# The load of w1 issued without a wait for x, and the low parts of all FFN weights made on GpSimd

## The chip, the cores and the metric

The kernel runs on one core of a Trainium2 chip. The metric is the device time of one execution in microseconds (us). Its engines are TensorE (PE in the profile), VectorE (DVE), ScalarE (ACT), GpSimd (POOL) and SyncE (SP); each works through its own list of instructions in order and waits on semaphores that the others raise. SP and ACT also issue DMA transfers, in order, from queues of their own (SPq, ACTq).

## The reference, cut to what matters

64 sequences ("tiles" below) of 128 tokens with 256 features go through gated cross attention (16 heads of 16, causal) and a gated FFN with a hidden width of 1024, of whose 16 blocks a router keeps 4 per token.

```python
def ffn(x, w_router, b_router, w1, b1, w2, b2):
    prob = softmax(xf @ w_router + b_router)
    mask = top 4 of the 16 blocks
    h = relu(xf @ w1b + b1b)
    y = einsum(h, w2b, mask) + b2
...
x = x + tanh(g_xattn[0]) * attention(_layernorm(x), ctx, ctx)
x = x + tanh(g_ffn[0]) * ffn(_layernorm(x), w_router, b_router, w1, b1, w2, b2)
```

All inputs are float32.

## The kernel before, in words

One tile is one sequence of 128 tokens. The work is a software pipeline over `ITERATIONS`, a loop variable i from -5 to 71 that every engine runs through on its own; "step i" below is one pass. The order on each engine is written out by hand, and semaphores tie the engines together.

In step i, PE makes the plain scores of tile i+1 (`scores`, L314), DVE takes their row maxima with a minus sign (`row_maximum`, L674 and L676), and these ride in `q_pad` of tile i+3 through PE's transpose (`q_transposed`, L283) and ACT's copy (`q_evacuated`, L504). SP moves them with two small DMAs into row 16 of each head's qT (`max_row`, L970). Then PE makes the scores of tile i again with the maximum subtracted (`shifted_scores`, L344), ACT takes the exponentials in two halves (`exponentials`, L525) and POOL zeroes what is above the diagonal (`causal_weights`, L873). Scores and shifted scores use the same four PSUM banks, so the next `scores` waits for the exponentials. `attention_out` (L357) and `out_transposed` (L371) follow one step later; DVE divides and adds the residual (`attention_added`, L684 to L694) and takes the statistics of the second layer norm. POOL makes the reciprocal roots of the variances, of x of tile i+4 and of the attention result of tile i-2 together (`roots`, L829 and L831). DVE normalises (`normalised`, L664, and `normalised_again`, L701, which makes `xn`), PE transposes `xn` (`x_transposed`, L382), ACT copies it to `xT` and, rounded, to `xT_high`, and DVE makes `xT_low` (`x_parts`, L707). Each second step has the router (L393, L401) with DVE's `route` (L746 to L758), ACT's `choice` (L569, `used`) and SP's transposing DMA of `used` (L1010).

The FFN matmuls are made from a rounded part ("high", type fp32r) and the rest ("low") of each operand, with three products: high by high, low by high, high by low. FFN work begins at step 5 (`hidden`, L423 to L425, then `ffn_out`, L446 to L448, from step 7).

The weights are split on the chip. w1 arrives by one DMA of 1 MB that ACT issues (L589). w2 arrives by eight DMAs on SP's queue (L1051) in the buffer that is later `hid`. They are cut into eight pieces of 128 x 512 elements, 0 to 3 of w1 and 4 to 7 of w2. ACT makes the high part of a piece by a copy (`weights_high`, L576), and then DVE (`weights_low`, L723) or POOL (`weights_low`, L887) the low part by a subtraction, in the step that `pieces_of` gives:

```python
def pieces_of(i):
    return {0: (0, 1), 1: (2, 3), 2: (4, 5), 3: (6,), 4: (7,)}.get(i, ())

W_LOW_BY_POOL = (0, 2, 4)
```

In POOL's loop `weights_low` comes behind `causal_weights` and `hidden_low`, at the end of a step, with `roots` of the next step behind it. In DVE's loop it comes behind `normalised_again` (steps up to 8) and before `layernorm_stats` of a later x. The first `hidden` on PE waits for four low parts, the first masked hidden piece on DVE (L738) and the first `ffn_out` for all eight.

x and the context stream in by DMAs of two tiles; at the start SP issues x of tiles 0, 1, 2 and 3 (L994 to L996), some small loads, then x of tiles 4 to 7 (L963).

Of the kernel before, what the change touches and what calls it, by code (L numbers as in the profile page):

```python
# [7 lines left out]
ALU = mybir.AluOpType  # L8
ACT = mybir.ActivationFunctionType
F32 = mybir.dt.float32  # L10
# [28 lines left out]
def build(nc, A_x, A_ctx, A_g_xattn, A_g_ffn, A_w_router, A_b_router, A_w1T, A_b1, A_w2T, A_b2, out):  # L39
# [24 lines left out]
    with ctx:  # L64
# [3 lines left out]
        def sem(name):  # L68
            return ctx.enter_context(nc.semaphore(name))
# [80 lines left out]
        x_landed = [sem(f"x_landed{i}") for i in range(XS // PAIR)]  # L150
# [30 lines left out]
        top_found, clipped_made, clipped_found, marked_made = (sem(n) for n in (  # L181
            "top_found", "clipped_made", "clipped_found", "marked_made"))

        w_low_also_made = sem("w_low_also_made")
        gated_b2_made, adding_made = sem("gated_b2_made"), sem("adding_made")

        ident16_zeroed, ident16_made, ident_zeroed, ident_made = (sem(n) for n in (
# [69 lines left out]
        def w_piece(n):  # L257
            turn = n % 4
            if n < 4:
                k, e = turn // 2, slice(turn % 2 * BLOCKS // 2, (turn % 2 + 1) * BLOCKS // 2)  # L260
                high, low = (t[:, k].rearrange("p c (e r) -> p e c r", e=BLOCKS)[:, e] for t in (w1_high, w1_low))
                return 0, w1_stage[:, k, e], high, low
            c = slice(turn * 2, turn * 2 + 2)
            return 1, w2_stage[:, c], w2_high[:, c], w2_low[:, c]

        def pieces_of(i):
            return {0: (0, 1), 1: (2, 3), 2: (4, 5), 3: (6,), 4: (7,)}.get(i, ())


        W_LOW_BY_POOL = (0, 2, 4)  # L270

        block = ctx.enter_context(nc.Block())

# [1 line left out]
        def _(pe):  # L275
# [128 lines left out]
            def hidden(p, m):  # L404
                ps = p % 2
                if m == 0:
                    pe.wait_ge(xT_low_made, p * PAIR + PAIR)
                if m == 0 and p == 0:
                    pe.wait_ge(k_copied, FFN_LAG + 2)
                    pe.wait_ge(w_low_made, 2)  # L410
                    pe.wait_ge(w_low_also_made, 2)
                n = PIECES * p + m
                if n > TAIL_PIECE:
                    pe.wait_ge(exp_done, 2 * N)
                    pe.wait_ge(hid_made, PC * (n - 1))
                elif n > 0:
                    pe.wait_ge(hid_made, PC * n)
                for j in range(PC):
                    c = PC * m + j
                    bank = hid_bank(n)[:, j * TOKS:(j + 1) * TOKS]  # L420
                    for k in range(KC):
                        high, low = (t[:, ps, k].rearrange("p t s -> p (t s)") for t in (xT_high, xT_low))
                        pe.matmul(out=bank, lhsT=w1_high[:, k, c], rhs=high, start=k == 0, stop=False)  # L423
                        pe.matmul(out=bank, lhsT=w1_high[:, k, c], rhs=low, start=False, stop=False)  # L424
                        made = pe.matmul(out=bank, lhsT=w1_low[:, k, c], rhs=high, start=False, stop=k == KC - 1)  # L425
                made.then_inc(hidden_made, 1)

            def ffn_out(b, half):
                p, t = divmod(b, PAIR)
                bank = out_bank(b)  # L430
                toks = slice(t * S, (t + 1) * S)
                if half == 0 and b >= TAIL_TILE:
                    pe.wait_ge(exp_done, 2 * N)
                    pe.wait_ge(y_made, b - 1)
                elif half == 0 and b >= 1:
                    pe.wait_ge(y_made, b)
                if half == 0 and b == 0:
                    pe.wait_ge(q_copied, QUERIES_BY_PE)
                    pe.wait_ge(w_low_made, 3)
                    pe.wait_ge(w_low_also_made, 5)  # L440
                if t == 0:
                    pe.wait_ge(h_low_made, PIECES * p + 2 * half + 2)
                for c in range(half * HC // 2, (half + 1) * HC // 2):
                    a, z = c == 0, c == HC - 1
                    high, low = h_high[:, p % 2, c, toks], h_low[:, p % 2, c, toks]
                    pe.matmul(out=bank[:, 0:D], lhsT=high, rhs=w2_high[:, c, :], start=a, stop=False)  # L446
                    pe.matmul(out=bank[:, 0:D], lhsT=high, rhs=w2_low[:, c, :], start=False, stop=False)  # L447
                    made = pe.matmul(out=bank[:, 0:D], lhsT=low, rhs=w2_high[:, c, :], start=False, stop=z)  # L448
                if half == 1:
                    made.then_inc(ffn_made, 1)  # L450
# [50 lines left out]
        def _(act):  # L501
# [83 lines left out]
            for u in range(U):  # L585
                rows = slice(u * PAD, (u + 1) * PAD)
                act.copy(tri[rows], triangle[rows, rows].unsqueeze(1).to_broadcast([PAD, HB, PAD])).then_inc(tri_made, 1)
            act.wait_ge(x_landed[1], 16)
            act.dma_start(w1_stage[:].rearrange("p k e c r -> p k (e c r)"),  # L589
                          A_w1T.rearrange("(k p) n -> p k n", p=P)).then_inc(w_landed[0], 16)  # L590
            def rest(i):
# [46 lines left out]
        def _(dve):  # L638
# [77 lines left out]
                dve.scalar_tensor_tensor(y_out[:, pair % 2, b % PAIR, :], out_bank(b)[:, 0:D], tanh_g[:, 1:2],  # L716
                                         x2_b2[:, b % GS, :], ALU.mult, ALU.add).then_inc(y_made, 1)

            def weights_low(i):
                for n in (n for n in pieces_of(i) if n not in W_LOW_BY_POOL):  # L720
                    _w, stage, high, low = w_piece(n)
                    dve.wait_ge(w_high_made, n + 1)
                    dve.tensor_tensor(low, stage, high.bitcast(F32), ALU.subtract).then_inc(w_low_also_made, 1)  # L723

            def hidden_masked(p, m):
                n = PIECES * p + m
                dve.wait_ge(hidden_made, n + 1)
                if n == 0:
                    dve.wait_ge(b1_landed, 16 * HC)
                    dve.wait_ge(w_low_made, 3)  # L730
                    dve.wait_ge(w_low_also_made, 5)
                if m == 0:
                    dve.wait_ge(used_turned, 16 * (p + 1))
                if n >= 4:
                    dve.wait_ge(h_low_made, n - 3)
                for j in range(PC):
                    c = PC * m + j
                    dve.scalar_tensor_tensor(hid[:, n % 4, j], hid_bank(n)[:, j * TOKS:(j + 1) * TOKS],  # L738
                                             b1_cols[:, c:c + 1], used_all[:, p % 2], ALU.add, ALU.mult
                                             ).then_inc(hid_made, 1)  # L740
# [33 lines left out]
            for i in ITERATIONS:  # L774
                pr, pu = router_pair(i), used_pair(i)
                p, m = hidden_pair(i)
                if 0 <= i - OUT_LAG - 1 < N:
                    finished(i - OUT_LAG - 1)
                if 0 <= i - 2 < N:
                    attention_added(i - 2)  # L780
                if 0 <= i + 3 < N:
                    normalised(i + 3)
                if 0 <= i + 1 < N:
                    row_maximum(i + 1)

                early = q_early(i)
                if early and 0 <= i - 2 < N:
                    normalised_again(i - 2)
                if p is not None:
                    hidden_masked(p, m)  # L790
                weights_low(i)
                if not early and 0 <= i - 2 < N:
                    normalised_again(i - 2)
                if 0 <= i + 5 < N:
                    layernorm_stats(i + 5)
                if i == FIRST + 1:
                    dve.wait_ge(place_zeroed, 1)
                    dve.wait_ge(ident16_made, 1)
                    places(0)
                    places(1)  # L800
                if 0 <= i - 3 < N:
                    x_parts(i - 3)
                if pr is not None:
                    route(pr)
                if i == FIRST + 2:
                    places(2)
                    places(3)
                if p is not None:
                    hidden_masked(p, m + 1)
                if i == FIRST + 2:  # L810
                    dve.wait_ge(ident_made, 1)
                    halves = ident[:].rearrange("p (t c e) -> p t c e", c=KC, e=PAD)
                    dve.tensor_tensor(adding[:], halves[:, :, 0], halves[:, :, 1], ALU.add).then_inc(adding_made, 1)
                if i == 0:
                    dve.wait_ge(small_landed, 16 * (KC + 1))
                    dve.wait_ge(tanh_done, 1)
                    dve.tensor_scalar(gated_b2[:], b2_all[:], tanh_g[:, 1:2], None, ALU.mult).then_inc(gated_b2_made, 1)

        @block.gpsimd
        def _(pool):  # L820
# [60 lines left out]
                                   ALU.subtract).then_inc(h_low_made, 1)  # L881

            def weights_low(i):
                for n in (n for n in pieces_of(i) if n in W_LOW_BY_POOL):
                    _w, stage, high, low = w_piece(n)
                    pool.wait_ge(w_high_made, n + 1)
                    pool.tensor_tensor(low, stage, high.bitcast(F32), ALU.subtract).then_inc(w_low_made, 1)  # L887
# [195 lines left out]
```

## Time and profile before

| | us |
|---|---|
| median of 3 runs | 681.2 |
| lowest, highest | 681.01, 684.17 |
| the profiled execution, its own time | 680.97 |
| its span | 679.1 |
| PE busy, share of the span | 659.7, 97% |
| DVE busy | 527.8, 78% |
| ACT busy | 538.9, 79% |
| POOL busy | 556.0, 82% |

The span is what the profiler sees from the first to the last instruction; the execution's own time holds a further 1.9 us around it. Busy shares are averages over the whole span. A row of a timeline gives start, duration, engine and line, the operation with its output and input, and in brackets how long the engine had been idle and what ended the idle time; a row with x2 holds two instructions in one. DMA issues are on SPq and ACTq. Line numbers are those of the kernel before.

### The profile page before, as it was taken

The page shows a single profiled execution, that of the slowest core. Times are in us where ns is not written, and L with a number is a line of the kernel's source. Part 1 is how long each engine was busy: PE and PEld are TensorE (multiplying, and loading weights), DVE is VectorE, ACT ScalarE, POOL GpSimd, SP SyncE. Part 2 cuts the span into 40 slices and gives each one's busy share as a digit, 9 for nine tenths or more (in the row PEclk, how much of TensorE's full clock was granted, in tenths as well). Part 3 has the DMA queues.
Part 4 walks back from the last instruction along what each step waited for, and adds up shares of the span by engine and source line. Part 5 has one row for each costly group of instructions (what it writes and reads, how often), then busy time and mean ns, then how long its engine had stood idle before and what let it go on. Part 6 is the DMA issues. An engine that isn't in the chain of part 4 may idle for free.

```text
span 679.1 us, 30579 instructions
## 1 busy us (share of the span) xinstructions
PE 659.7 (97%) x12960; PEld 611.9 (90%) x12960; DVE 527.8 (78%) x1429; ACT 538.9 (79%) x785; POOL 556.0 (82%) x718
## 2 busy tenths in 40 slices
PE   6779999999999999999999999999999999999997
PEld 5668899999999999999999999989999999999997
DVE  6899887788777778788778878777878877877742
ACT  4668788888888888888888888888888888887732
POOL 6677888988988898888898898888888889887643
PEclk9899999999999999999999999999999999999999
DMA  5323355556545446645556654544554554553110
GB/s 197 96 55 86 88 109 99 116 109 115 120 114 116 99 110 116 111 112 113 100 117 107 116 111 122 103 107 114 113 113 112 116 100 96 98 86 64 28 40 32
DMA packets 192279, 69.24 MB, mean 102 GB/s; under 512 B 166160, under 2 KB 191888, under 8 KB 192144
## 3 DMA queue, kind: packets, MB, share of 16 engines
q1 hardware_dynamic: 191312, 65.72, 45.7%
q8 instruction: 102, 1.67, 1.1%
q10 hardware_dynamic: 832, 1.57, 0.6%
q14 instruction: 33, 0.27, 0.1%
HBM read 19.03 MB, written 8.39 MB: 40 GB/s over the span
## 4 chain that ended last, share of the span: by engine, by line
PE 86%; DVE 5%; DMA 3%; ACT 2%; issue 2%; POOL 1%; SPq 1%; POOLq 0%; DVEq 0%
PE bank L423 11%; PE score_banks L344 10%; PE bank L357 8%; PE score_banks L314 8%; PE bank L425 8%; PE bank L424 8%; PE bank L446 8%; PE bank L447 8%; PE bank L448 8%; PE bank L371 4%; PE bank L401 2%; PE score_banks L327 1%; DMA used_all<-used 1%; PE bank L393 1%; ACT weights L525 1%
## 5 line engine op out<-in xcount | busy, mean ns | idle before, releaser
L880 POOL TENSOR_TENSOR h_low<-hid,h_high 128x512 fp32r<-128x512 f32 x128 | 164.2, 1283 | 12.8 <-ACT hid L560 12.8
L738 DVE SCALAR_TENSOR_TENSOR hid<-bank,b_cols,used_all 128x256 f32<-128x256 f32 x248 | 108.1, 477 | 65.9 <-PE bank L425 58.2
L873 POOL TENSOR_SCALAR_AFFINE_SELECT weights<-weights 128x1024 f32<-128x1024 f32 x128 | 138.2, 1103 | 18.2 <-ACT weights L525 16.4
L423 PE MATMUL bank<-xT_high,w_high 128*128 128x256 f32 x496 | 151.5, 305 | 0.8 <-DVE hid L738 0.7
L525 ACT ACTIVATE weights<-score_banks 128x1024 f32<-128x1024 f32 x128 | 124.3, 1024 | 34.7 <-PE score_banks L344 34.6
L424 PE MATMUL bank<-xT_low,w_high 128*128 128x256 f32 x496 | 139.4, 281 | 0.0
L425 PE MATMUL bank<-xT_high,w_low 128*128 128x256 f32 x496 | 139.4, 281 | 0.0
L446 PE MATMUL bank<-w_high,h_high 128*128 128x256 f32 x488 | 137.3, 281 | 0.7 <-POOL h_low L880 0.7
L447 PE MATMUL bank<-w_low,h_high 128*128 128x256 f32 x488 | 137.7, 282 | 0.0
L448 PE MATMUL bank<-w_high,h_low 128*128 128x256 f32 x488 | 136.2, 279 | 0.0
L423 PEld LDWEIGHTS bank<-xT_high,w_high 128*128 128x128 f32 x496 | 93.3, 188 | 8.9 <-DVE hid L738 1.1
L424 PEld LDWEIGHTS bank<-xT_low,w_high 128*128 128x128 f32 x496 | 93.5, 189 | 0.0
L425 PEld LDWEIGHTS bank<-xT_high,w_low 128*128 128x128 f32 x496 | 93.3, 188 | 0.0
L446 PEld LDWEIGHTS bank<-w_high,h_high 128*128 128x128 f32 x488 | 91.8, 188 | 0.9 <-POOL h_low L880 0.9
L448 PEld LDWEIGHTS bank<-w_high,h_low 128*128 128x128 f32 x488 | 92.2, 189 | 0.0
L447 PEld LDWEIGHTS bank<-w_low,h_high 128*128 128x128 f32 x488 | 91.8, 188 | 0.0
L519 ACT COPY kT<-kT_parts 128x1024 uint16<-128x1024 uint16 x57 | 77.9, 1366 | 16.1 <-DMA kT_parts<-k_parts 15.8
L559 ACT ACTIVATE h_high<-hid 128x512 fp32r<-128x512 f32 x128 | 80.8, 631 | 9.9 <-DVE hid L738 9.9
L344 PE MATMUL score_banks<-qT,kT 32*128 32x128 f32 x2048 | 75.1, 283 | 6.6 <-DMA qT<-qT 3.6
L513 ACT COPY qT<-qT_parts 128x1024 uint16<-128x1024 uint16 x57 | 77.6, 1361 | 4.1 <-DMA qT_parts<-q_parts 3.7
L344 PEld LDWEIGHTS score_banks<-qT,kT 32*128 32x128 f32 x2048 | 63.0, 186 | 19.6 <-issue 12.7
L560 ACT ACTIVATE hid<-hid 128x512 f32<-128x512 f32 x128 | 80.3, 628 | 0.0
(105 smaller groups left out, 1411.1 us busy)
## 6 DMA issues: line engine op xcount, KB each, us to landing
x_in<-in_x SPq DMA_DIRECT2D x31, 256.0 KB, 3.1
out_y<-y_out SPq DMA_DIRECT2D x31, 256.0 KB, 2.2
c_in<-in_ctx SPq DMA_DIRECT2D x30, 256.0 KB, 2.8
qT<-qT SPq DMA_DIRECT2D x128, 4.0 KB
w_stage<-in_w1T ACTq DMA_DIRECT2D x1, 1024.0 KB, 9.2
hid<-in_w2T SPq DMA_DIRECT2D x8, 128.0 KB, 2.7
kT_parts<-k_parts SPq DMA_TRANSPOSE x57, 2.8
qT_parts<-q_parts SPq DMA_TRANSPOSE x57, 2.7
```

The source lines that it names most:

```text
L344: made = pe.matmul(out=score_banks[:, u, cols], lhsT=kT[rows, s, cols], rhs=qT[rows, s, cols], start=True, stop=True, tile_position=(u * P ...
L423: pe.matmul(out=bank, lhsT=w1_high[:, k, c], rhs=high, start=k == 0, stop=False)
L424: pe.matmul(out=bank, lhsT=w1_high[:, k, c], rhs=low, start=False, stop=False)
L425: made = pe.matmul(out=bank, lhsT=w1_low[:, k, c], rhs=high, start=False, stop=k == KC - 1)
L446: pe.matmul(out=bank[:, 0:D], lhsT=high, rhs=w2_high[:, c, :], start=a, stop=False)
L447: pe.matmul(out=bank[:, 0:D], lhsT=high, rhs=w2_low[:, c, :], start=False, stop=False)
L448: made = pe.matmul(out=bank[:, 0:D], lhsT=low, rhs=w2_high[:, c, :], start=False, stop=z)
L525: act.activation(weights[:, b % 2, half * 2 * HB:(half + 1) * 2 * HB, :].rearrange("p h q -> p (h q)"), score_banks[:, 2 * half:2 * half + ...
L559: act.activation(h_high[:, p % 2, chunks], hid[:, n % 4], ACT.Relu)
L738: dve.scalar_tensor_tensor(hid[:, n % 4, j], hid_bank(n)[:, j * TOKS:(j + 1) * TOKS], b1_cols[:, c:c + 1], used_all[:, p % 2], ALU.add, AL ...
L873: pool.affine_select(out=w, in_=w, compare_op=ALU.is_ge, fill=0.0, base=0, pattern=[[0, 2 * HB], [1, S]], channel_multiplier=-1).then_inc( ...
L880: pool.tensor_tensor(h_low[:, p % 2, chunks], hid[:, n % 4], h_high[:, p % 2, chunks].bitcast(F32), ALU.subtract).then_inc(h_low_made, 1)
```

## The change

ACT issues the DMA of w1 without waiting for x of tiles 2 and 3. POOL makes all eight low parts. The pieces come in the order 1, 2, 2, 2, 1 over steps 0 to 4, for ACT's high parts too. The semaphore of DVE's low parts goes, and the waits for both semaphores become waits for one.

```diff
@@ -264,10 +263,8 @@
         def pieces_of(i):
-            return {0: (0, 1), 1: (2, 3), 2: (4, 5), 3: (6,), 4: (7,)}.get(i, ())
-
-
-        W_LOW_BY_POOL = (0, 2, 4)
+            return {0: (0,), 1: (1, 2), 2: (3, 4), 3: (5, 6), 4: (7,)}.get(i, ())
@@ -407,8 +404,7 @@
                 if m == 0 and p == 0:
                     pe.wait_ge(k_copied, FFN_LAG + 2)
-                    pe.wait_ge(w_low_made, 2)
-                    pe.wait_ge(w_low_also_made, 2)
+                    pe.wait_ge(w_low_made, 4)
@@ -436,8 +432,7 @@
                     pe.wait_ge(q_copied, QUERIES_BY_PE)
-                    pe.wait_ge(w_low_made, 3)
-                    pe.wait_ge(w_low_also_made, 5)
+                    pe.wait_ge(w_low_made, 8)
@@ -585,7 +580,6 @@
-            act.wait_ge(x_landed[1], 16)
             act.dma_start(w1_stage[:].rearrange("p k e c r -> p k (e c r)"),
@@ -716,19 +710,12 @@
-            def weights_low(i):
-                for n in (n for n in pieces_of(i) if n not in W_LOW_BY_POOL):
-                    _w, stage, high, low = w_piece(n)
-                    dve.wait_ge(w_high_made, n + 1)
-                    dve.tensor_tensor(low, stage, high.bitcast(F32), ALU.subtract).then_inc(w_low_also_made, 1)
-
             def hidden_masked(p, m):
...
-                    dve.wait_ge(w_low_made, 3)
-                    dve.wait_ge(w_low_also_made, 5)
+                    dve.wait_ge(w_low_made, 8)
@@ -788,7 +775,6 @@
-                weights_low(i)
@@ -881,7 +867,7 @@
             def weights_low(i):
-                for n in (n for n in pieces_of(i) if n in W_LOW_BY_POOL):
+                for n in pieces_of(i):
```

POOL's order from the masks of step 2 to those of step 4, before (`weights` are the exponentials that are masked, `ve` and `rstd` are made by `roots`, `x_b` is x2_b2, the residual with the gated bias):

```order
L873 AFFINE_SELECT weights<-weights 128x1024 x2
L887 TENSOR_TENSOR w_low<-hid,w_high 128x512
L829 TENSOR_SCALAR ve<-mv 128x2
L831 TENSOR_TENSOR rstd<-ve,half_power 128x2
L919 TENSOR_TENSOR x_b<-x,gated_b 128x256
L839 COPY v_pad<-c_in 128x16x16
L873 AFFINE_SELECT weights<-weights 128x1024 x2
L829 TENSOR_SCALAR ve<-mv 128x2
L831 TENSOR_TENSOR rstd<-ve,half_power 128x2
```

and the same stretch of the change:

```order
L859 AFFINE_SELECT weights<-weights 128x1024 x2
L873 TENSOR_TENSOR w_low<-w_stage,w_high 128x8x8x8
L873 TENSOR_TENSOR w_low<-hid,w_high 128x512
L815 TENSOR_SCALAR ve<-mv 128x2
L817 TENSOR_TENSOR rstd<-ve,half_power 128x2
L905 TENSOR_TENSOR x_b<-x,gated_b 128x256
L825 COPY v_pad<-c_in 128x16x16
L859 AFFINE_SELECT weights<-weights 128x1024 x2
L873 TENSOR_TENSOR w_low<-hid,w_high 128x512 x2
L815 TENSOR_SCALAR ve<-mv 128x2
L817 TENSOR_TENSOR rstd<-ve,half_power 128x2
```

One low part more stands before `roots` of step 3, and two before `roots` of step 4, where there were none. Step 1 also has one more before `roots` of step 2, and step 4 one where there was none.

DVE's order from the maxima of step 3 to the router of step 4, before:

```order
L676 TENSOR_REDUCE q_pad<-score_banks 128x4x2
L701 TENSOR_SCALAR xn<-x,mv,rstd 128x256
L723 TENSOR_TENSOR w_low<-hid,w_high 128x512
L645 BN_STATS stats<-x_in 128x6
L647 BN_AGGR mv<-stats 128x2
L707 TENSOR_TENSOR xT_low<-xT,xT_high 128x2x128
L684 RECIPROCAL gain<-bank 128x16
```

and the same stretch of the change:

```order
L670 TENSOR_REDUCE q_pad<-score_banks 128x4x2
L695 TENSOR_SCALAR xn<-x,mv,rstd 128x256
L639 BN_STATS stats<-x_in 128x6
L641 BN_AGGR mv<-stats 128x2
L701 TENSOR_TENSOR xT_low<-xT,xT_high 128x2x128
L678 RECIPROCAL gain<-bank 128x16
```

The low part behind `xn` is gone there, as it is in steps 0, 1, 2 and 4.

## Rows read from the trace of the kernel before

**Rows 1.** The page: TensorE's busy time in all, and its granted clock by slice.

```profile
PE 659.7 (97%) x12960; PEld 611.9 (90%) x12960; DVE 527.8 (78%) x1429; ACT 538.9 (79%) x785; POOL 556.0 (82%) x718
...
PEclk9899999999999999999999999999999999999999
```

**Rows 2.** The chain that ended last, 0 to 70 us: start, us, what.

```profile
1.72 4.84 DMA x_in<-in_x
...
13.41 2.62 DMA qT<-qT
...
34.78 1.31 POOL w_low L887
...
37.14 0.80 DVE xn L701
37.94 0.80 DVE w_low L723
...
47.44 1.80 SPq L1010
...
49.90 1.62 DMA qT<-qT
```

**Rows 3.** The timeline of POOL.

```profile
36.06 0.23 POOL L829 TENSOR_SCALAR ve<-mv 128x2 f32<-128x2 f32 x1
...
41.76 0.25 POOL L829 TENSOR_SCALAR ve<-mv 128x2 f32<-128x2 f32 x1
...
49.39 0.23 POOL L829 TENSOR_SCALAR ve<-mv 128x2 f32<-128x2 f32 x1 [1.11 <-DVE mv L647]
...
56.01 1.28 POOL L880 TENSOR_TENSOR h_low<-hid,h_high 128x512 fp32r<-128x512 f32 x1
```

**Rows 4.** The timeline of DVE.

```profile
12.56 0.43 DVE L645 BATCH_NORM_STATS2 stats<-x_in 128x6 f32<-128x256 f32 x1 [1.27 <-DMA x_in<-in_x]
...
30.23 0.81 DVE L701 TENSOR_SCALAR xn<-x,mv,rstd 128x256 f32<-128x256 f32 x1 [0.36 <-POOL rstd L831]
...
32.31 0.23 DVE L684 RECIPROCAL gain<-bank 128x16 f32<-128x16 f32 x1
...
43.59 0.41 DVE L701 TENSOR_SCALAR xn<-x,mv,rstd 128x256 f32<-128x256 f32 x1
43.91 1.09 DVE L723 TENSOR_TENSOR w_low<-hid,w_high 128x512 fp32r<-128x512 f32 x1
...
56.10 1.47 DVE L691 SCALAR_TENSOR_TENSOR x<-att,tanh_g,x_in 128x256 f32<-128x256 f32 x1
```

**Rows 5.** The timeline of PE (matmuls).

```profile
16.07 1.17 PE L344 MATMUL score_banks<-qT,kT 32*128 32x128 f32 x32 [2.28 <-DMA qT<-qT]
...
31.25 0.44 PE L382 MATMUL bank<-ident,xn 128*128 128x128 f32 x2
31.52 0.60 PE L371 MATMUL bank<-ident,oT 128*128 128x128 f32 x4
...
46.47 0.63 PE L371 MATMUL bank<-ident,oT 128*128 128x128 f32 x4 [0.95 <-issue]
```

**Rows 6.** The timeline of ACT at the start.

```profile
7.00 0.58 ACT L508 COPY kT<-bank 128x512 f32<-128x512 f32 x1 [2.15 <-DMA x_in<-in_x]
...
15.75 1.14 ACT L576 CAST w_high<-w_stage 128x512 fp32r<-128x512 f32 x2 [1.33 <-DMA w_stage<-in_w1T]
```

**Rows 7.** Instructions of line 691: duration in ns, min/median/max.

```profile
L691 DVE SCALAR_TENSOR_TENSOR x<-att,tanh_g,x_in x64: 484/580/1470, 25.8 to 645.6; 128x256 f32<-128x256 f32 x64
```

**Rows 8.** Busy time by stretch: length, PE, PEld, DVE, ACT, POOL, granted clock, DMA.

```profile
17.00:18.00 1.00, 1.00 (x17) 0.88 (x10) 0.97 (x3) 0.69 (x1) 0.00 (x0) 0.76 0.66 210
18.00:20.00 2.00, 1.48 (x31) 1.11 (x36) 1.65 (x3) 2.00 (x4) 1.59 (x2) 0.50 0.46 140
20.00:22.00 2.00, 2.00 (x98) 1.82 (x82) 0.72 (x1) 1.25 (x3) 2.00 (x3) 0.77 0.05 12
...
28.00:30.00 2.00, 0.81 (x32) 0.54 (x20) 1.87 (x3) 1.00 (x2) 1.92 (x3) 1.00 0.30 84
```

More of the change, by code:

```diff
@@ L182, in build @@
             "top_found", "clipped_made", "clipped_found", "marked_made"))
-        w_low_also_made = sem("w_low_also_made")
         gated_b2_made, adding_made = sem("gated_b2_made"), sem("adding_made")
```

## The prediction

> **What bounds the kernel now.** I read the page first. TensorE (PE) is busy for 97% of the span and its clock is full in all slices but the first two [rows 1]. So once PE has a full queue, nothing on the other engines that the change touches can shorten the run; they can only start PE later. I then looked for the stretch in which PE is not the chain. That is the ramp, roughly the first 50 us, in which attention runs alone and the FFN matmuls have not begun. The chain of waits there runs through the landing of x for tiles 2 and 3, a small transfer for qT, then GpSimd's (POOL's) low part of weight piece 4, VectorE's (DVE's) normalisation `xn` behind it, and DVE's own low part of a piece [rows 2]. Both kinds of instruction that the change moves are therefore on the chain: the POOL one for 1.31 us, the DVE one for 0.80 us. A microsecond lost in the ramp is lost at the end, since the PE work behind it is fixed; one gained there is gained.
>
> In the timeline of POOL the reader is to see that `roots` (L829) starts right behind the low part, with no idle time in front of it, in the steps where POOL makes one [rows 3]. In DVE's, `xn` waits for POOL's rstd in step 2 (0.36 us idle), but not in step 4 [rows 4]. I number the steps by the loop variable i; a number in brackets behind an operation is its tile.
>
> **The change, part by part.**
>
> *The load of w1 without its wait.* ScalarE (ACT) could issue it only when x of tiles 2 and 3 had landed, at 1.72 + 4.84 = 6.56 [rows 2]. ACT's next copy came at 7.00 after 2.15 us of idle time, so ACT was free at about 4.85 [rows 6]. The load goes out some 1.7 us sooner. The first use of w1 is at 15.75 [rows 6], but the exponentials behind it in ACT's queue wait for PE's scores, and these for the qT transfer that lands at 16.03 [rows 2]. So an earlier w1 frees nothing by itself. ACT's first copy can come up to 0.9 us sooner; the chain does not go through it, but through x of tiles 2 and 3 and DVE [rows 2]. I take 0. Bounds: a gain if the 2.62 us of the qT transfer were partly the tail of w1's traffic; it cannot shrink below the 1.62 us of a later one [rows 2], and DVE's maxima for the next scores end at about 15.25, so at most 0.8 us. A loss if w1's bytes now delay x of tiles 2 and 3 (on the chain one for one), or x of tiles 4 and 5, for which DVE already waits 1.27 us at 12.56 [rows 4]. With the load issued 1.7 us sooner I bound that loss at 1.3 us. It is nearest to nothing, since x of tiles 2 and 3 has landed 1.7 us after the new issue, and even a qT transfer of 4 KB took 1.62 and 2.62 us [rows 2].
>
> *Low parts, five of them moved from DVE to POOL.* A piece costs POOL 1.3 us [rows 2] and costs DVE 0.80 us in step 3 and, at 1.09 less a little overlap, 1.0 in step 4 [rows 2, 4]. POOL has now 1, 2, 2, 2, 1 pieces in steps 0 to 4 where it had 1, 1, 1, 0, 0. Only what it delays behind it counts.
>
> Step 1, one piece more. It ends 1.3 us later, and rstd with it, so `xn`(0) starts at 31.53 instead of 30.23 and, at its 0.81 us, ends at 32.35. PE's transposes of it (L382) stood at 31.25 [rows 5] and go to 32.4, 1.15 late, with the transposes of the attention output (L371) behind them. The piece that leaves DVE does not help, because DVE's next work, the reciprocal at 32.31 [rows 4], waits for L371. Before, that one had ended at 31.52 + 0.60 = 32.12 [rows 5]; now 33.27. So **+1.0 us** for the reciprocal and all DVE work up to the maxima of tile 4, on which PE's shifted scores of tile 3 wait.
>
> Step 2, one piece more. The causal masks in front are bound by the exponentials, which are not late yet. So `roots` goes from 36.06 [rows 3] to about 37.45, and `xn`(1) is 1.4 late. DVE loses its own 0.80 us [rows 2], which leaves 0.6; and all that waits for the exponentials of tile 3 is already 1.0 late. The larger counts: **still +1.0 us**, of which I carry 0.95.
>
> Step 3, two pieces where there were none. `roots`(4) started at 41.76 with nothing in front of it to wait for [rows 3]; it goes to 41.76 + 0.95 + 2.6 = 45.3. From `roots` to `xn` it takes 1.08 us (36.06 to 37.14) [rows 2, 3], so `xn`(2) goes from 43.59 [rows 4] to 46.4, 2.8 late. It will run beside the POOL addition that always follows rstd, as those at 30.23 and 37.14 did, in 0.80 instead of 0.41 us: +0.4. DVE's own piece leaves: -1.0. So the statistics behind it, at 44.9, go to 47.1, **+2.2 us** in all. Behind them in DVE stand xT_low and the router's chain. PE's L371 at 46.47 (0.95 us idle before it) [rows 5] waits for the router's clipped logits, `used` waits for the marks, SP's transposing transfer of 1.80 us at 47.44 waits for `used`, and the qT transfer that releases the scores at 51.5 stands behind that one in SP's queue [rows 2]. All of this is on the chain, so the 2.2 us pass through it whole.
>
> Step 4, one piece more. `roots`(5) had waited 1.11 us for DVE [rows 3], and DVE is 2.2 us late itself, so only 0.1 to 0.2 us of the 1.3 show, on an rstd that DVE takes up later. The first masked hidden piece needs the eighth low part, made at about 51.7, and comes at about 53.7. I cost it at 0; what hides it is POOL's idle time and DVE's maxima.
>
> ACT's high parts move by one piece a step. At about 0.6 us each [rows 6] they fall before ACT's waits for PE, so 0.
>
> *What more POOL work does to DVE.* L691 takes 0.58 us in the median but 1.47 at 56.10, where a POOL instruction started at 56.01 runs to 57.29; DVE's ends 0.28 us after it [rows 3, 4, 7]. `xn` takes 0.81 beside POOL work and 0.41 at 43.59 [rows 4]. So DVE instructions with SBUF operands stand until POOL's current one has ended. The POOL work I add is 6.5 us, most of it in steps 2 to 4 of the chain. By the timeline as moved above, L691 in step 3 and the normalisation behind it each meet a POOL instruction with 0.1 to 0.8 us still to run. Bounds: 0, and about 1.2 us (the 0.9 us by which 1.47 exceeds the median, and the 0.3 of a second one). I take 0.5.
>
> The Trainium skill ("SBUF — State Buffer", Who interferes with whom) states that these two engines share a port pair as an exclusive lock, for DVE instructions with two SBUF inputs or in a two-port mode, and that reductions never take it. By that rule DVE's maxima, 1.8 us a tile, would pay nothing and L691 would; the trace agrees for L691 with its 1.47 us. Without the lock the sum would be 2.2 us, with it 2.7.
>
> **The sum:** 0 + 2.2 + 0.5 = 2.7 us over the profiled execution's 680.97 us, 683.7. The median of the runs is 0.2 above that execution, so I predict **683.9 us**, +0.4%. About 0.5%, or 3.4 us, is what a measurement of this kernel can tell from no change, so this counts as "same", near its upper edge.
>
> **Rivals.**
>
> *The POOL work is mostly hidden, or the start pays it back.* For it: POOL has idle time (1.11 us at 49.39), and an earlier w1 may shorten the qT transfer by up to 0.8. Against: the chain goes through the low part at 34.78, and `roots` has no idle time before it at 36.06 and 41.76. It gives +0 to +1.9 us, 682.2. Chance 0.22.
>
> *TensorE's clock falls in the ramp, and the kernel is slower by more than 0.5%.* Place: from the end of the shifted scores of tile 4 (about 46) to L371 at about 48.7 PE has only L382 and the router's two small matmuls to do. Before, the granted clock went from 2.4 GHz towards 1.2 between 17 and 22 (0.76, 0.50, 0.77) after PE had stood for 2.3 us before the scores at 16.07 [rows 5, 8]. Its price by those rows: 0.24 + 1.0 + 0.46 = 1.7 us of full clock, and it would now meet the first FFN matmuls, which fill PE. It gives 2.7 + 1.7 = 4.4, 685.6. It decides once that idle stretch is as empty as the earlier one. Against it: with PE busy for 0.81 of the 2 us from 28 to 30 the clock stayed at 1.00 [rows 8]. Chance 0.15.
>
> The skill ("TensorE: Matmul & The Clock Gate", HAM oscillation) holds that waits that leave the array idle bring the slow clock back; in this trace it fell once, behind the longest gap.
>
> *More contention than I took.* The x loads land up to 1.3 us late behind w1, or DVE meets POOL more often (1.2 instead of 0.5), or SP's key transfer, which POOL's later key parts now release only just before `used`, holds up the 1.80 us transfer. It gives 3.5 to 5, 685.2. Chance 0.16.
>
> *Faster by over 0.5%.* DVE would have to be the bound of the ramp alone. But only its pieces of steps 3 and 4 cost the chain anything, 0.80 and 1.0 us, and POOL's lie there too. Chance 0.02.
>
> The forecast itself (2.0 to 3.4 us) has 0.45. The range leaves out the lower part of the first rival and the cases in which the last two costs come together: 681.9 to 686.3. Chances: faster 0.02; same 0.45 + 0.22 - 0.01 = 0.66; slower 0.15 + 0.16 + 0.01 = 0.32.
>
> **What would show it.** In the changed profile: L817 (rstd) of step 2 ends at about 31.5 and releases `xn`; `xn` of step 4 waits about 1.8 us for POOL, where it had waited for nothing; the shifted scores at 51.5 come at about 54.2; from there on every PE instruction keeps that distance to the end; x of tiles 2 and 3 still lands at about 6.6. I am wrong if w1's earlier traffic moves the scores at 16.07 by more than 0.5 us either way, if the clock shows a second dip, or if the distance at 51.5 is under 1.5 us.

## The result and the profile after

The changed kernel takes 689.39 us (median of 4 runs, 687.22 to 690.12) against 681.95 for the kernel before, measured together with it (4 runs, 681.01 to 684.17): a ratio of 1.0102, 95% interval 1.008 to 1.0124. That is 7.4 us slower, outside the range of the prediction and on the slower side of its 0.5%. The profiled execution took 687.22 us with a span of 685.4, so this pair of profiles holds 6.3 us of the loss.

The page of the changed kernel, its busy time and PE's clock, to be read against [rows 1]:

```profile
PE 661.6 (97%) x12960; PEld 614.3 (90%) x12960; DVE 523.4 (76%) x1424; ACT 539.4 (79%) x785; POOL 562.2 (82%) x723
...
PEclk9898999999999999999999999999999999999999
```

PE has the same 12960 matmuls. They take 1.9 us more, and there is a second slice, the fourth, in which the clock is not full. After the ramp no more is lost: the distance is 7.0 us at the exponentials of tile 5 and 6.3 at the end, so the loss arises in the first 60 us, as the prediction had it. The start of ACT's exponentials of each tile, and of `used`, from the timelines of ACT, shows where (e1, e2 and e10 are experiments told below):

| us | tile 0 | 1 | 2 | 3 | 4 | `used` | 5 | span |
|---|---|---|---|---|---|---|---|---|
| before | 17.31 | 24.48 | 31.39 | 38.17 | 45.04 | 46.91 | 52.80 | 679.1 |
| the change | 20.21 | 27.03 | 34.00 | 41.93 | 48.71 | 51.83 | 59.75 | 685.4 |
| e1, load alone | 20.14 | 26.90 | 33.95 | 40.75 | 47.61 | 49.48 | 55.40 | 681.6 |
| e2, POOL alone | 16.82 | 24.09 | 31.13 | 39.85 | 47.76 | 49.75 | 57.81 | 684.8 |
| e10, POOL alone, PE kept busy | 17.43 | 24.21 | 31.18 | 39.10 | 46.46 | 49.19 | 55.59 | 682.9 |

The change is 2.9 us late at tile 0, 2.6 at tiles 1 and 2, 3.8 and 3.7 at tiles 3 and 4 and 7.0 at tile 5. Three things stand behind these steps.

**The start.** The chain of the changed kernel, in order of time (start, us, what), begins differently from [rows 2]:

```profile
4.58 3.85 SPq L991
...
8.48 0.81 SPq L991
...
9.33 5.87 DMA x_in<-in_x
...
15.22 0.44 DVE stats L639
```

Before, the chain went through x of tiles 2 and 3. Now it goes through SP's own issue of two small loads (L991, w_router) and then x of tiles 4 and 5. SP's timeline shows the same, and ACT's shows w1's load:

```profile
3.65 0.89 SPq L989 DMA_DIRECT2D br_rows<-in_b_router  x2
4.58 4.71 SPq L991 DMA_DIRECT2D w_router<-in_w_router  x2
9.33 1.50 SPq L949 DMA_DIRECT2D x_in<-in_x  x2
```

```profile
3.53 0.41 ACTq L583 DMA_DIRECT2D w_stage<-in_w1T  x1
3.62 1.24 ACT L582 COPY tri<-triangle 32x128 bf16<-32x128 bf16 x4
```

The two issues took 0.90 us in the kernel before and take 4.71. The loads of x behind them go out at 9.33 instead of 5.53. The load of w1 itself left at 3.53, before ACT's four copies that stand ahead of it in the program. In the kernel before it left at 6.58, so this is 3 us sooner and not the 1.7 I had read. The order has turned round with it: before, w1's load went out behind the loads of x of tiles 4 to 7, and now it goes out ahead of them. In DVE's timeline the statistics of tile 4 then wait 3.46 us for x and start 2.7 us later than in [rows 4], and in PE's the shifted scores of tile 0 come at 18.06 against 16.07 in [rows 5]:

```profile
15.22 0.43 DVE L639 BATCH_NORM_STATS2 stats<-x_in 128x6 f32<-128x256 f32 x1 [3.46 <-DMA x_in<-in_x]
```

```profile
18.06 2.09 PE L341 MATMUL score_banks<-qT,kT 32*128 32x128 f32 x32 [3.80 <-DVE q_pad L670]
```

Those scores take 2.09 us instead of 1.17: PE had been idle for 3.8 us and is at half clock.

**POOL.** Its low parts stand in the chain twice, with `roots` and `xn` behind them, and `xn` waits 1.56 and 1.57 us for POOL in DVE's timeline, against 0.36 and nothing in [rows 4]:

```profile
30.42 2.53 POOL w_low L873 x2
...
33.23 0.74 POOL rstd L817
...
34.00 0.81 DVE xn L695
...
45.33 2.54 POOL w_low L873 x2
...
48.14 0.74 POOL rstd L817
...
48.90 0.81 DVE xn L695
```

```profile
34.00 0.80 DVE L695 TENSOR_SCALAR xn<-x,mv,rstd 128x256 f32<-128x256 f32 x1 [1.56 <-POOL rstd L817]
...
48.90 0.80 DVE L695 TENSOR_SCALAR xn<-x,mv,rstd 128x256 f32<-128x256 f32 x1 [1.57 <-POOL rstd L817]
```

**The clock.** Busy time by stretch (length, PE, PEld, DVE, ACT, POOL, granted clock, DMA), to be read against [rows 8]:

```profile
16.00:18.00 2.00, 0.00 (x0) 0.00 (x0) 2.00 (x4) 0.00 (x0) 1.17 (x3) 0.50 0.89 293
18.00:20.00 2.00, 1.94 (x32) 1.83 (x32) 1.00 (x4) 0.00 (x0) 0.00 (x0) 0.50 0.66 210
20.00:22.00 2.00, 2.00 (x12) 1.57 (x8) 0.00 (x0) 1.79 (x2) 0.70 (x1) 0.50 0.03 4
...
48.00:50.00 2.00, 0.89 (x26) 0.70 (x22) 1.10 (x2) 1.29 (x2) 1.92 (x5) 1.00 0.34 116
50.00:52.00 2.00, 1.20 (x7) 1.04 (x6) 1.76 (x13) 0.82 (x2) 2.00 (x3) 0.50 0.02 6
52.00:54.00 2.00, 2.00 (x41) 1.67 (x41) 1.41 (x3) 0.96 (x3) 2.00 (x2) 0.50 0.74 165
54.00:56.00 2.00, 2.00 (x68) 1.83 (x56) 1.93 (x5) 1.38 (x3) 0.80 (x3) 0.50 0.04 4
56.00:58.00 2.00, 2.00 (x30) 1.86 (x33) 1.77 (x4) 0.48 (x1) 1.85 (x4) 0.80 0.04 10
```

There are two falls from 2.4 to 1.2 GHz: the first is longer than before, and the second, from 50 to 57 us, is new. PE was idle from 14.3 to 18.06 us, and the first fall comes inside this stretch (the mean from 14 to 16 us is 0.96, then 0.50). Before the second PE was busy for 0.89 of 2 us. The second meets the first FFN matmuls, which fill PE: three stretches at 0.50 and one at 0.80 lose 3.4 us of full clock.

### The profile page after: what moved, and what is told of

Its sections match the earlier page's. It is cut to its first block, busy times and chain, and to the rows that moved or that the text cites. A ratio compares the mean times of both kernels' runs of the same rounds, so it can differ in the third digit from the quotient of the medians.

```text
span 685.4 us, 30577 instructions
## 1 busy us (share of the span) xinstructions
PE 661.6 (97%) x12960; PEld 614.3 (90%) x12960; DVE 523.4 (76%) x1424; ACT 539.4 (79%) x785; POOL 562.2 (82%) x723
## 3 DMA queue, kind: packets, MB, share of 16 engines
q10 hardware_dynamic: 832, 1.57, 0.6%
HBM read 19.03 MB, written 8.39 MB: 40 GB/s over the span
## 4 chain that ended last, share of the span: by engine, by line
PE 86%; DVE 4%; DMA 3%; POOL 2%; SPq 2%; issue 1%; ACT 1%; POOLq 0%; DVEq 0%
PE bank L419 11%; PE score_banks L341 10%; PE bank L354 8%; PE score_banks L311 8%; PE bank L420 8%; PE bank L421 8%; PE bank L442 8%; PE bank L441 8%; PE bank L443 8%; PE bank L368 4%; PE bank L398 2%; PE score_banks L324 1%; DMA used_all<-used 1%; PE bank L390 1%; DMA x_in<-in_x 1%
## 5 line engine op out<-in xcount | busy, mean ns | idle before, releaser
L514 ACT COPY kT<-kT_parts 128x1024 uint16<-128x1024 uint16 x57 | 77.7, 1363 | 14.5 <-DMA kT_parts<-k_parts 14.4
L668 DVE TENSOR_REDUCE q_pad<-score_banks 128x8 f32<-128x1024 f32 x64 | 78.0, 1219 | 4.8 <-PE score_banks L324 4.8
L815 POOL TENSOR_SCALAR ve<-mv 128x2 f32<-128x2 f32 (+1 forms) x70 | 16.3, 233 | 78.9 <-DVE mv L641 78.9
```

## Experiments

All are compared with the kernel before, run on the same chip together with them; its medians there were 681.95 (27 runs, for e1 to e4), 682.25 (26, for e5 to e8) and 682.15 (23, for e9 and e10). A loss in us is the difference of two medians. The ratio, with its 95% interval in brackets, is estimated on its own and gives up to 1.1 us less; 0.001 of it is 0.7 us.

### e1: only w1's load is sent early

```diff
-            act.wait_ge(x_landed[1], 16)
             act.dma_start(w1_stage[:].rearrange("p k e c r -> p k (e c r)"),
```

> The kernel before with w1's load issued without its wait, and nothing else. Theory Q (the early load holds up SP's next DMA issues, so x of tiles 4 to 7 is issued 3.8 us later): one of SP's two w_router issues again takes about 4 us, statistics of tile 4 start at about 15.2 instead of 12.6, the shifted scores of tile 0 at about 18.1 instead of 16.1, the exponentials of tile 3 at about 40.7 instead of 38.2; total +2.5 to +3. No second fall of the clock near 50 us. Rival P (the whole loss of 6.3 us is POOL's): total within 0.5 us of the kernel before.

Measured: 685.94 us, ratio 1.0052 (1.0037 to 1.0067). SP's timeline, and the statistics of tile 4 in DVE's:

```profile
4.58 5.13 SPq L1004 DMA_DIRECT2D w_router<-in_w_router  x2
9.76 2.22 SPq L962 DMA_DIRECT2D x_in<-in_x  x2
```

```profile
15.47 0.43 DVE L644 BATCH_NORM_STATS2 stats<-x_in 128x6 f32<-128x256 f32 x1 [4.03 <-DMA x_in<-in_x]
```

The row of e1 in the table is 2.4 to 2.6 us late from tile 1 to tile 5 and has no fall of the clock near 50 us. What theory Q expected of the trace came; the median, +4.0 (+3.5 by the ratio), is above the +2.5 to +3 I had given. The profiled run was the quickest of e1's ten, with a mean clock of 0.997 against 0.995 over all ten, so the rest may be the clock; that is not shown. The load without its wait, which I had costed at nothing, is about half of the loss.

### e2: only the low parts move

```diff
+            act.wait_ge(x_landed[1], 16)
             act.dma_start(w1_stage[:].rearrange("p k e c r -> p k (e c r)"),
```

(in the changed kernel)

> The change with the wait for x of tiles 2 and 3 put back: only the low parts move. Theory Q+P: start as before (shifted scores of tile 0 at 16.1), xn of step 2 ends 1.3 us late, exponentials of tile 3 at about 39.3 (+1.1), L371 before the router's marks at about 48.8 (+2.3), and then either no second fall of the clock (total +2.3) or a fall behind the idle stretch at 46 to 49 (total +4). Rival S (the start does it all): total within 0.5 us of the kernel before.

Measured: 686.71 us, ratio 1.0061 (1.0042 to 1.008), +4.8, where I had given +4 with a second fall of the clock. The start is as before, the second fall of the clock is there. In this profile it also fell between 38 and 42 us, behind POOL's delay of step 2. Two causes, then, of 4.0 and 4.8 us; they sum to 8.8 where the change measures 7.4, and each of the three is known to 1 to 1.5 us either way.

### e3: e1 with the loads of x in front

```diff
+            load_x(4)
+            load_x(6)
             sync.dma_start(gates[:, 0:1], A_g_xattn.partition_broadcast(P)).then_inc(gates_landed, 16)
...
-                    if 2 * PAIR <= i + X_AHEAD < N:
+                    if 4 * PAIR <= i + X_AHEAD < N:
```

> e1 with SP's loads of x of tiles 4 to 7 issued right behind those of tiles 2 and 3, before gates, b2, router bias and w_router. Theory Q (issues are held up, and only x matters): SP's w_router issue still takes about 4 us but delays nothing on the chain; statistics of tile 4 start no later than in the kernel before (12.6) and perhaps at once behind the maxima (11.4); total -1 to +0.3 against the kernel before. Rival B (the bytes of w1 compete with x in the DMA engines): x of tiles 4 and 5 still lands at about 15, and the total stays at +2.5.

Measured: 682.81 us, ratio 1.0006 (0.9991 to 1.0021). SP's timeline:

```profile
2.19 0.98 SPq L962 DMA_DIRECT2D x_in<-in_x  x2
3.21 0.47 SPq L998 DMA_DIRECT2D gates<-in_g_xattn  x1
3.72 0.43 SPq L999 DMA_DIRECT2D gates<-in_g_ffn  x1
4.20 0.77 SPq L1000 DMA_DIRECT2D b_all<-in_b  x1
5.00 1.15 SPq L1004 DMA_DIRECT2D br_rows<-in_b_router  x2
6.20 1.11 SPq L1006 DMA_DIRECT2D w_router<-in_w_router  x2
```

With w1's load sent as early as in e1 the loss is gone (+0.9, not clear of zero). So it hangs on whether x of tiles 4 to 7 is sent ahead of w1's load or behind it. It does not show what delays x behind w1: here x goes ahead both in SP's queue and in the transfers themselves, so rival B, that x waits for the bytes of w1, is not excluded by this run. One expectation missed: the long issue did not move to another load; it is spread over three small ones (0.77, 1.15, 1.11) or absent. Why the order of SP's queue decides this stays open.

### e5: e1 with the w_router loads behind those of x

```diff
+            load_x(4)
+            load_x(6)
             for c in range(KC):
                 sync.dma_start(w_router[:, c, 0:BLOCKS], A_w_router[c * P:(c + 1) * P, :]).then_inc(small_landed, 16)
...
-                    if 2 * PAIR <= i + X_AHEAD < N:
+                    if 4 * PAIR <= i + X_AHEAD < N:
```

> e1 (only w1's load sent early) with SP's two w_router loads moved behind its loads of x of tiles 4 to 7, everything else in SP's queue as it was. e1 had 5.13 us for the two w_router issues at 4.58. Theory Q1 (whatever SP issues at that moment is held up by w1's load): the x issue at 4.58 now takes 4 to 5 us, statistics of tile 4 start at 14 to 15.5, total +2.5 to +4 as in e1. Theory Q2 (the w_router loads with their 64 byte rows are what is held up): x is issued by 5.6, statistics of tile 4 start by 12.6, the stall, if any, falls behind, total within 1 us of the kernel before.

Measured: 684.51 us, ratio 1.0028 (1.0011 to 1.0044), +2.3. SP's timeline, and the row of x in the chain:

```profile
4.59 4.43 SPq L962 DMA_DIRECT2D x_in<-in_x  x2
9.06 1.46 SPq L1006 DMA_DIRECT2D w_router<-in_w_router  x2
```

```profile
4.59 11.44 DMA x_in<-in_x
```

Now the x loads take the 4.43 us and the w_router loads do not. What is held up is whatever SP issues at that moment, about 1 us after w1's load has left: theory Q1. But the statistics of tile 4 start at 16.05, later than the 14 to 15.5 expected and later than in e1, although both x issues are over at 9.02, before e1 begins its own at 9.76. So the time at which SP issues x does not by itself set the time at which it lands.

### e9: half of w1 early, half behind the wait

```diff
-            act.wait_ge(x_landed[1], 16)
-            act.dma_start(w1_stage[:].rearrange("p k e c r -> p k (e c r)"),
-                          A_w1T.rearrange("(k p) n -> p k n", p=P)).then_inc(w_landed[0], 16)
+            act.dma_start(w1_stage[:, 0].rearrange("p e c r -> p (e c r)"), A_w1T[0:P]).then_inc(w_landed[0], 16)
+            act.wait_ge(x_landed[1], 16)
+            act.dma_start(w1_stage[:, 1].rearrange("p e c r -> p (e c r)"), A_w1T[P:2 * P]).then_inc(w_landed[0], 16)
```

> The kernel before with w1's load cut in two of 512 KB: the first is sent without a wait (at about 3.5), the second behind the wait for x of tiles 2 and 3. Theory A (the hold-up of SP's issues grows with the size of the load that is under way): SP's issues at 4.58 and 5.5 take 0.4 to 0.5 us each as in the kernel before or up to 2 us in all, x of tiles 4 and 5 lands at 12.5 to 13.5, total 0 to +1. Rival (any load of w1 from ACT at 3.5 holds up SP for 4 us): statistics of tile 4 at 15 to 16, total +2.5 to +4.

Measured: 685.16 us, ratio 1.0037 (1.0017 to 1.0058), +3.0. SP's timeline:

```profile
3.72 3.13 SPq L1003 DMA_DIRECT2D br_rows<-in_b_router  x2
6.89 1.46 SPq L1005 DMA_DIRECT2D w_router<-in_w_router  x2
8.39 1.58 SPq L963 DMA_DIRECT2D x_in<-in_x  x2
```

My theory A falls. The six issues from 3.72 on take 6.2 us where they took 2.7 in the kernel before, and x goes out at 8.39. That is only 1 us sooner than with the whole load early, and the statistics of tile 4 started no sooner, at 15.56. The hold-up of the issues does not shrink in proportion to the load. For the landing of x this run is no test of the size: the second half left at 6.87, so the whole of w1 was still ahead of x.

The kernels side by side (start of the issue, and landing, in us; from the timelines of SP and ACT and the times from issue to landing; for e9 the second half of w1 is given):

| | x of tiles 4, 5 issued | w1 issued | x landed | w1 landed |
|---|---|---|---|---|
| before | 5.53 | 6.58 | 12.5 | 15.8 |
| e3 | 2.19 | 3.53 | 8.6 | 12.1 |
| the change | 9.33 | 3.53 | 15.2 | 14.4 |
| e1 | 9.76 | 3.51 | 15.5 | 14.6 |
| e5 | 4.59 | 3.51 | 16.0 | 15.5 |
| e9 | 8.39 | 6.87 | 15.5 | 15.0 |

Where x is sent ahead of w1, it lands before it. Where it is sent behind, it lands 0.5 to 0.9 us after w1, whether its issue begins at 4.59 or at 9.76. So the loss goes with x standing behind w1, and the long issue does not explain by itself how late x lands. What holds x back there stays open; the DMA engines were not full in the hold-up (busy for 0.11 to 0.25 of their time from 6 to 8 us in the change, e1 and e5).

### e4: e2 with POOL's low parts in front of the masks

```diff
+                weights_low(i)
                 if 0 <= i < N:
                     causal_weights(i)
                 if p is not None:
                     hidden_low(p, m)
-                weights_low(i)
```

> e2 with POOL's low parts in front of the masks of a step instead of behind them, so that they fall into POOL's wait for the exponentials (3.8, 2.5, 1.2 and 1.1 us idle in steps 0 to 3 before). Theory P (the low parts hurt because roots of the next step stand behind them with no idle time between): roots(2) and roots(3) come at their old times or up to 1.3 us sooner than in e2, roots(4) about 1.5 late instead of 2.6+; total +0 to +1. Rival L (two engines' port contention or the number of pieces is what costs, wherever they stand): total as e2.

Measured: 683.73 us, ratio 1.001 (0.9989 to 1.0031), +1.8 instead of +4.8 (by the ratio +0.7, not clear of zero; I had given 0 to +1). POOL's timeline from step 2 to step 4:

```profile
31.21 1.27 POOL L874 TENSOR_TENSOR w_low<-w_stage,w_high 128x512 fp32r<-128x512 f32 x1
32.43 1.32 POOL L874 TENSOR_TENSOR w_low<-hid,w_high 128x512 fp32r<-128x512 f32 x1
36.62 0.25 POOL L816 TENSOR_SCALAR ve<-mv 128x2 f32<-128x2 f32 x1
38.66 2.83 POOL L874 TENSOR_TENSOR w_low<-hid,w_high 128x512 fp32r<-128x512 f32 x2
43.74 0.25 POOL L816 TENSOR_SCALAR ve<-mv 128x2 f32<-128x2 f32 x1
```

The same eight pieces on the same engine cost 3.0 us less where they fall into POOL's wait for the exponentials. `roots` of step 4 starts 3.6 us after the exponentials of tile 3 (40.16), against 5.9 in e2 (45.75 and 39.85) and 3.6 in the kernel before. From the exponentials of tile 2 to those of tile 5 e4 takes 21.6 us, the kernel before 21.4, e2 26.7 and e10 (below, e2 with the clock kept up) 24.4. So it is the place in POOL's queue, in front of `roots`, that costs, and not the work. In this profile the clock was low between 8 and 12 and between 24 and 30 us instead.

### e6: the change, with PE kept busy

Idle transposes of the identity, which nothing reads, go to a PSUM bank that is free there.

```diff
+            def filler(bank, n):
+                for _ in range(n):
+                    pe.transpose(banks[bank][:, 0:P], ident[:], ident[:])
...
+                if i == 0:
+                    filler(M0, 24)
                 if 0 <= i < N:
                     shifted_scores(i)
...
+                if i == 4:
+                    pe.wait_ge(k_copied, KEYS_BY_PE)
+                    filler(HID_BANK, 10)
                 if 0 <= i - 2 < N and x_by_pe(i - 2):
                     x_transposed(i - 2)
...
+                if i == 4:
+                    filler(HID_BANK, 7)
                 if 0 <= i - 1 < N:
                     out_transposed(i - 1)
```

> The change as a whole, with idle transposes of the identity on PE whose result nothing reads: 24 in front of the shifted scores of tile 0, 10 in front of the transposes of xn and 7 in front of those of the attention output in step 4. Theory C (TensorE's clock falls behind those idle stretches and this costs some 2 to 3 us of the change's 7.4): mean clock about 0.997 to 1.0 instead of 0.99, no fall between 48 and 58 us, median 2 to 3 us under the change's 689.4. Rival W (the waits alone cost it, the clock is a companion): median within 0.7 us of the change's.

Measured: 686.51 us, ratio 1.0066 (1.0044 to 1.0088), 2.9 us under the change, with more work on PE. Busy time by stretch:

```profile
18.00:20.00 2.00, 1.95 (x40) 1.86 (x40) 0.99 (x4) 0.72 (x1) 0.00 (x0) 1.00 0.66 209
...
50.00:52.00 2.00, 2.00 (x23) 1.66 (x22) 1.42 (x12) 1.12 (x2) 2.00 (x3) 1.00 0.57 132
52.00:54.00 2.00, 2.00 (x88) 1.93 (x88) 1.90 (x4) 1.93 (x4) 1.18 (x1) 1.00 0.21 45
54.00:56.00 2.00, 1.84 (x39) 1.43 (x38) 2.00 (x4) 0.58 (x2) 1.62 (x4) 1.00 0.02 4
```

The falls at 16 and 50 us are gone. (One between 40 and 46, where I had put nothing, was there in this profile.) The mean clock over its runs is 0.997 against 0.991 for the change. The two medians were measured at different times, against 681.95 and 682.25 for the kernel before, and with the two intervals the 2.9 us are known to about 2 us either way. The profiles agree with theory C: from the exponentials of tile 4 to those of tile 5 this kernel takes 8.89 us (48.67 to 57.56) and the change 11.04.

### e10: e2 with PE kept busy

e2 with such transposes: 16 in front of the shifted scores of tile 0, 8 in front of those of tile 3, 10 and 7 in step 4 as in e6.

> e2 (only the low parts moved to POOL, the wait kept, +4.8) with idle transposes on PE: 16 in front of the shifted scores of tile 0, 8 in front of those of tile 3, 10 and 7 in step 4. If the prediction's terms for POOL are right (2.2 of waits and 0.5 of contention) and the clock is the rest: mean clock 0.997 or more, total +2.2 to +3 against the kernel before. If the waits are mis-sized: +4 or more at a clock of 0.997.

Measured: 685.16 us, ratio 1.0033 (1.0014 to 1.0051), +3.0 between the medians, mean clock 0.997. Its profile has the full clock throughout; the stretch that holds e2's second fall, in e2 and in e10:

```profile
48.00:52.00 4.00, 2.97 (x51) 2.53 (x54) 3.20 (x15) 2.92 (x5) 3.58 (x4) 0.53 0.39 87
52.00:56.00 4.00, 4.00 (x87) 3.69 (x79) 3.84 (x8) 1.66 (x3) 2.79 (x6) 0.61 0.04 7
```

```profile
48.00:52.00 4.00, 4.00 (x105) 3.60 (x104) 3.53 (x15) 3.05 (x6) 3.20 (x3) 1.00 0.39 86
52.00:56.00 4.00, 3.27 (x75) 2.78 (x74) 3.97 (x10) 1.26 (x3) 2.60 (x5) 1.00 0.01 2
```

Counted from the exponentials of tile 1, `used` is 2.6 us late (24.98 against 22.43) and the exponentials of tile 5 are 3.1 late (31.38 against 28.32). This is what the moved low parts cost when the clock does not fall, and the sum had 2.7 for it. (The median, +3.0, is +2.3 by the ratio, from 1.0 to 3.5 us.)

### e7: the change with both causes mended, and e8: a try at a faster kernel

e7 is the changed kernel with SP's order of e3 and POOL's order of e4.

> The change with both suspected causes mended: SP's loads of x of tiles 4 to 7 in front of the small loads (as in e3, +0.9 alone instead of +4.0), POOL's low parts in front of the masks (as in e4, +1.8 instead of +4.8). If the two causes are separate and are the whole of it: +1 to +3 against the kernel before. If something else of the change costs time: +5 or more.

Measured: 682.64 us, ratio 1.0006 (0.9988 to 1.0024). This is +0.4 us, under the +1 to +3 expected. The change's two parts, put elsewhere in two queues, cost nothing that can be measured; whatever else the change does costs less than the interval's 1.6 us.

e8 is the kernel before with POOL's three pieces in front of the masks and 16 idle transposes in front of the shifted scores of tile 0.

> The kernel before with POOL's three low parts in front of the masks, and 16 idle transposes in front of the shifted scores of tile 0. Theory C+P: roots(3) starts about 1.2 us sooner (34.9), xn(1) no longer waits for POOL, and the fall of the clock between 17 and 22 us goes: median 0.5 to 1.5 us under the kernel before, mean clock 0.998 or more. Rival (these are hidden in the kernel before): within 0.4 us.

Measured: 682.62 us, ratio 1.0004 (0.9984 to 1.0024), mean clock 0.995. No gain, where I had expected 0.5 to 1.5 us: `xn` of step 3 no longer waits for POOL, but the maxima and the exponentials bound the step, and in its profile the clock fell between 8 and 13 us instead. No version was faster than the kernel before.

## Why the prediction was wrong

**What bounds it** held: the loss is all in the ramp, and the PE work behind it is unchanged. One reading was off: only the second slice of the page shows less than the full clock, not the first two. Of the three signs of being wrong that the prediction named, two came: the scores at 16.07 moved by 2.0 us, and the clock fell a second time.

**The load of w1 without its wait** is the step that failed. It said "I take 0" and bounded a loss at 1.3 us; measured alone it costs 4.0 (e1). Three readings in it were wrong. First, the time of the issue: I took ACT's next copy as the moment when ACT was free, but a DMA issue does not stand behind ACT's copies, and it left at 3.53 and not at 4.85. Second, the order: the wait had kept w1's load at 6.58, behind the loads of x of tiles 4 to 7 at 5.53, and without it the load goes ahead of them. I named the delay of x behind w1 as a possible loss but took it as nearest to nothing. The runs show x landing 0.5 to 0.9 us after w1 in all four kernels in which it is sent behind it, and no measurable loss with x in front (e3). I also never asked whether w1's load would hold up SP's *issues*; it did, by 3.8 us in the change and 4.2 in e1, but in e5 x is as late although its issue begins at 4.59. Third, the bound of 1.3 us rested on "1.7 us sooner": the load went out 3.0 us sooner, and the statistics of tile 4 started 2.7 us later, the shifted scores of tile 0 2.0 later. Of x of tiles 2 and 3, which I had feared for, the statistics started at 7.04 instead of 6.58.

**The low parts on POOL** were right, step by step, as long as the clock does not fall. For step 1 it said `xn` 1.3 us late and +1.0 for what follows; in e10, counted from the exponentials of tile 1, `xn` is 1.2 late and the exponentials of tile 3 are 1.2. For step 3 it said `xn` 2.8 late and +2.2 at `used`, with 0.5 of contention put down apart; e10 has 2.75 and 2.6. Step 4's piece was hidden, as costed: `roots` of step 5 still waits 1.12 us for DVE.

**Contention** of 0.5 us was not tested alone. The rows fit: in the changed kernel L685 (L691 before) takes 1.00 and 0.90 in steps 3 and 4 against 0.83 and 0.57, xT_low 0.62 against 0.39, and the first part of the maxima 1.21 to 1.23 in both. That last is as the Trainium skill says ("SBUF — State Buffer", Who interferes with whom): a reduction never takes the shared port pair. The maxima read PSUM, though, so these rows do not show what a reduction of an SBUF operand would do.

**The clock** was among the rivals, with its place, its mechanism and a price of 1.7 us, and only 0.15 of the chance. It came, at that place. From the exponentials of tile 4 to those of tile 5 the changed kernel takes 11.04 us, e10 9.13 and the kernel before 7.76, so the second fall cost 1.9 us in that profile. The medians give 1.6 us for POOL's part (e2 and e10, by themselves not clear of zero) and 2.9 for the whole (e6). This is the second term that was missing: with the clock kept up the change costs 4.3 us, not 7.4. The chance was mis-sized because I asked whether one idle stretch was as empty as another. The moment at which the clock falls varies from profile to profile: e3's has no fall, e8's one at 8 us, the kernel before one at 17. Where no transposes are added, the slower kernels tend to have the lower mean clock, and the mean clock of a kernel's runs (0.9965 before, 0.995 for e1, 0.992 for e2, 0.991 for the change) tells it better than one profile does.

The 6.95 us at tile 5 of the profile can be split so: 2.0 from x standing behind w1, 0.9 from the slow clock in front of tile 0 (e6, which keeps it up, starts those exponentials at 19.28 instead of 20.21) less 0.35, since the kernel before had its own slow clock between tiles 0 and 1 (7.17 us against 6.82 here and 6.77 in e3), 1.2 from POOL in steps 1 and 2, -0.1 between tiles 3 and 4, then 1.4 from POOL and 1.9 from the clock between tiles 4 and 5.

## What to carry to other kernels

Before a large transfer is sent earlier, write down what the other issuing engine puts in its queue in the next few microseconds: which transfers were ahead of the large one and will now be behind it? Send what the chain needs in front of it. Work for an idle engine is free only at the place in its queue where it idles: the same pieces cost 4.8 us behind the masks and 1.8 or less in front of them. In a stretch where TensorE waits, add the price of a slow clock to every new wait, by the mean clock of many runs and not by one profile.

## What the runs showed of the hardware that was not expected

A load of 1 MB issued by ACT at 3.5 us made SP's next issues take 4.4 to 5.1 us for a pair (e1, e5, the change) instead of 0.9; half of it, 3.1 us (e9). Issued at 6.6, when SP had nothing to issue before 12.7, it held up nothing. With SP's x loads issued before it, SP's next issues took 0.7 to 0.8 us for one and 1.1 to 1.2 for a pair, and none was held up for long (e3, e7). What fills up is not shown. A load of x issued behind it landed 0.5 to 0.9 us after it, however early its own issue began. The Trainium skill ("DMA: Bandwidth & Descriptors", Issuing engines are not separate DMA queues) says that transfers run on the same 16 engines whichever engine starts them, and that a second issuing engine only saves the time of the issue, usually small beside the transfer. The trace does not agree on the size: in the change the pair of w_router issues took 4.71 us, about as long as the 5.87 us from issue to landing of x.

ACT's DMA issue left its queue before four copies that stand ahead of it in the program (3.53 against copies from 3.62 to 4.86; 3.49 to 3.53 in all six kernels that issue w1's load, or half of it, without the wait). So the opening's "in order" does not hold between ACT's DMA issues and its copies.
